# Expert tiles' down product as five fp32r products over 128 and 48 rows, the high and low parts of the 48 loaded tile by tile

## What is computed

```python
x = x + L0_ffn(L0_cond(x, itok, ...))     # top 2 of 8 experts, capacity, width 176
# second layer, on h = LoRA-SwiGLU(x) of 256 -> 1024 -> 256
probs = softmax(h @ router_w.T)                        # 16 experts
top_vals, top_idx = top_k(probs, 4)                    # normalised to sum 1
g = einsum('nh,ehi->eni', h, w_gate)                   # i = 176
u = einsum('nh,ehi->eni', h, w_up)
y = einsum('eni,eih->enh', silu(g) * u, w_down)        # the down product, 176 -> 256
routed = einsum('enh,ne->nh', y, comb)
shared = silu(h @ sh_gate) * (h @ sh_up) @ sh_down     # width 704
x = x + routed + sigmoid(h @ sh_gate_w) * shared
```

## Time and profile before

| | |
|---|---|
| three executions | 388.51, 390.02, 390.42 us (median 390.02) |
| the profiled execution | 390.62 us, of which the span is 388.8 |
| TensorE busy | 363.8 us, 94% of the span |
| VectorE busy | 227.2 us, 58% |
| GpSimd busy | 177.6 us, 46% |
| ScalarE busy | 143.4 us, 37% |
| mean granted TensorE clock | .988 of full speed |
| DMA | 53.98 MB, 139 GB/s over the span |

### The profile page before, as it was taken

One profiled execution on the slowest core, in us unless ns is written; L12 is line 12 of the kernel. 1 busy time (PEld: TensorE's weight loads), 2 busy tenths in 40 slices (PEclk: granted clock), 3 DMA queues, 4 the chain that ended last, 5 costly groups with the idle time before them and its releaser, 6 DMA issues.

```text
span 388.8 us, 6306 instructions
## 1 busy us (share of the span) xinstructions
PE 363.8 (94%) x1961; PEld 313.0 (81%) x1961; DVE 227.2 (58%) x556; ACT 143.4 (37%) x292; POOL 177.6 (46%) x162
## 2 busy tenths in 40 slices
PE   3998899999999999999999989989999999999992
PEld 3877789887888888888868768779999999999871
DVE  6796557269822222221247897775766566566696
ACT  2653466334444343333333715543222222232110
POOL 0606664566064445424222115763443344177783
PEclk9999999999999999999998999999999999999998
DMA  7985255145962134310111058752443444255633
GB/s 223 370 317 176 77 168 187 58 161 177 385 242 94 45 132 135 135 40 3 40 40 42 1 176 174 186 170 78 129 109 110 124 112 114 88 162 165 190 97 121
DMA packets 26949, 53.98 MB, mean 139 GB/s; under 512 B 4278, under 2 KB 16054, under 8 KB 26582
## 3 DMA queue, kind: packets, MB, share of 16 engines
q1 hardware_dynamic: 21686, 39.28, 30.8%
q0 software_dynamic: 5232, 14.29, 13.4%
HBM read 40.19 MB, written 15.47 MB: 143 GB/s over the span
## 4 chain that ended last, share of the span: by engine, by line
PE 73%; DVE 10%; DMA 6%; issue 3%; POOL 3%; ACT 2%; SPq 1%; POOLq 0%; DVEq 0%; ACTq 0%
PE gu L1552 10%; PE y L1944 10%; PE gu L1554 10%; PE gu L1553 10%; PE gu L1916 4%; PE gu L1920 4%; PE gu L1917 4%; PE y L1552 2%; PE y L1553 2%; PE y L1554 2%; PE gu L1578 2%; DMA xgT_f<-y_k,slot_s 2%; PE gu L1928 2%; DMA w_raw<-y_k 1%; PE gu L1865 1%
## 5 line engine op out<-in xcount | busy, mean ns | idle before, releaser
L616 POOL TENSOR_TENSOR w_lo<-w_raw,w_hi 128x768 fp32r<-128x768 f32 (+3 forms) x26 | 34.4, 1344 | 77.9 <-ACT w_hi L750 60.7
L1053 DVE TENSOR_TENSOR hid<-silu,gu 128x512 f32<-128x512 f32 x24 | 16.5, 686 | 66.1 <-PE gu L1554 66.0
L1552 PE MATMUL gu<-act_hi,w_hi 128*128 128x512 f32 x128 | 52.9, 413 | 1.5 <-DVE hid L1053 1.5
L1553 PE MATMUL gu<-act_lo,w_hi 128*128 128x512 f32 x128 | 51.0, 399 | 0.0
L1554 PE MATMUL gu<-act_hi,w_lo 128*128 128x512 f32 x120 | 48.1, 401 | 0.0
L978 ACT ACTIVATE silu<-gu 128x176 f32<-128x176 f32 x47 | 14.9, 317 | 72.2 <-PE gu L1920 72.2
L1916 PE MATMUL gu<-w_hi,xgT 128*128 x94 | 38.7, 413 | 0.8 <-ACT xgT L933 0.8
L1434 DVE TENSOR_TENSOR hid<-silu,gu 128x176 f32<-128x176 f32 x47 | 15.8, 337 | 37.5 <-ACT silu L978 34.9
L779 ACT ACTIVATE hid_hi<-hid 128x512 fp32r<-128x512 f32 x24 | 15.2, 632 | 49.1 <-DVE hid L1053 49.0
L1552 PEld LDWEIGHTS gu<-act_hi,w_hi 128*128 128x128 f32 x128 | 24.8, 194 | 7.1 <-DVE hid L1053 2.0
L1917 PE MATMUL gu<-w_lo,xgT 128*128 x94 | 30.1, 321 | 0.0
(11 more groups left out here) (354 smaller groups left out, 917.6 us busy)
## 6 DMA issues: line engine op xcount, KB each, us to landing
y_k<-w_raw SPq DMA_DIRECT2D x47, 128.0 KB, 2.2
w_raw<-in_w_gu SPq DMA_DIRECT2D x16, 352.0 KB, 4.6
w_raw<-in_wc SPq DMA_DIRECT2D x8, 576.0 KB, 4.0
w_hi_f<-in_w0s SPq DMA_DIRECT2D x6, 368.0 KB, 4.8
y_k<-hid SPq DMA_DIRECT2D x1, 2048.0 KB, 12.3
w_dn<-in_w_dn SPq DMA_DIRECT2D x1, 1936.0 KB
w_raw<-in_ws SPq DMA_DIRECT2D x5, 384.0 KB, 3.0
w_hi_f<-y_k SPq DMA_DIRECT2D x6, 256.0 KB, 4.4
```

Source lines behind the costliest of these rows:

```text
L616: nc.gpsimd.tensor_tensor(w_lo[par][:, w], w_raw[par][:, w], w_hi[par][:, w].bitcast(F32), ALU.subtract).then_inc(split, 1)
L1053: V.tensor_tensor(out[rows(tail)], silu[s][rows(tail)], up[rows(tail)], ALU.mult).then_inc(s_prod, 1)
L1552: T.matmul(out, w[0], x[0], start=start, stop=False)
L1553: T.matmul(out, w[0], x[1], start=False, stop=False)
```

## The change

The down product of a tile (176 x 256) is no longer two fp32 products over 88 rows each. The 176 rows are cut into 128 and 48. The 128 rows have a high and a low part in SBUF, side by side in lora_store, made once (by ScalarE and GpSimd, `w1_dn_high`, `w1_dn_low`), in two instructions each, of 11 and 5 experts. The 48 rows stand for each expert in a new DRAM array w1_rest of 128 rows by 256, with the high part from row 0 and the low part from row 64. It is made during COND in four pieces of four experts (`rest_load`, `rest_high`, `rest_low`, `rest_store`) in the buffers sg_b and xgT, and the piece of a tile's expert is loaded for every tile by SyncE (`rest_in`, 128 KB, the address from a register) into a ring of three and rounded by VectorE (`round_rest`) into one of two. Hidden is written by VectorE as 128 columns and, at column 128 and again 64 further, the last 48. The turned hidden part gets a high part from ScalarE (`hid_turned_high`, from PSUM) and a low part from VectorE (a subtraction, PSUM less SBUF); its ring has three places instead of four. The result is copied to t_out by ScalarE (`output`) instead of VectorE. Choice gathers open one tile earlier (Y_OPEN 31).

```diff
-Y_OPEN, Y_A_TILE = 32, 2
+Y_OPEN, Y_A_TILE = 31, 2
...
+TURNED, REST_RING, REST_BACK = 3, 3, 3
...
# SyncE
+            def rest_load(k):
+                if k:
+                    sp.wait_ge(rest_low_done, ES + k)
+                n = REST_EXP * H
+                sp.dma_start(sg_b[:], d["w1_dr"][:, k * n:(k + 1) * n]).then_inc(rest_landed, 16)
+
+            def rest_store(k):
+                sp.wait_ge(rest_low_done, ES + k + 1)
...
             for c in range(C0[COND] + 2, C0[COND] + NC[COND]):
                 cond_chunk(c, c % 2)
+                k = c - C0[COND] - 2
+                if 1 <= k <= REST_PIECES:
+                    rest_store(k - 1)
+                if k < REST_PIECES:
+                    rest_load(k)
...
+            def rest_in(i):
+                e = sp.value_load(own[0:1, i:i + 1], min_val=0, max_val=E1 - 1)
...
                 sp.dma_start(d["y_k"][i * P:(i + 1) * P], t_out[i % RING]).then_inc(s_y[i % RING], 16)
+                if i + REST_RING + 1 < SLOT_TILES:
+                    sp.wait_ge(rest_rounded, ES + i + 2)
+                    rest_in(i + REST_RING + 1)
                 if i:
                     landed(i - 1)
...
# GpSimd
+            def w1_dn_low(k):
+                of = slice(*WD_EXPERTS[k])
+                pool.wait_ge(s_w1h, NC[COND] + k + 1)
+                nc.gpsimd.tensor_tensor(w1_dn_lo[:, of], w1_dn_raw[:, of], w1_dn_hi[:, of].bitcast(F32),
+                                        ALU.subtract).then_inc(s_w1l, 1)
...
-            for i in range(9, SLOT_TILES):
+            w1_dn_low(0)
+            for i in range(9, XG):
+                gather(i, i)
+            w1_dn_low(1)
+            for i in range(XG, SLOT_TILES):
                 gather(i, i % XG)
...
# ScalarE
+                if 2 <= k < 2 + REST_PIECES:
+                    rest_high(k - 2)
...
             gu1_high(last_cols(1))
+            w1_dn_high(0)
             shared(3, 0)
             act.wait_ge(s_ids, 1)
             turned_in(0)
             shared(3, 1, lambda: turned_in(1))
+
+            w1_dn_high(1)
+
+            def hid_turned_high(i):
+                act.wait_ge(t_hT, i + 1)
+                if i >= TURNED:
+                    act.wait_ge(t_dn, i - TURNED + 1)
+                A.activation(t_hidT[i % TURNED][0], hidT_ps(i), ACT.Copy).then_inc(t_hh, 1)
...
# VectorE
+                if 2 <= k < 2 + REST_PIECES:
+                    rest_low(k - 2)
...
-                V.tensor_tensor(t_hid[i % DEPTH], t_silu[i % 2], tile_gu(i)[:, I_EXP:GU_N], ALU.mult).then_inc(t_hd, 1)
...
+                V.tensor_tensor(out[:, 0:I_EXP], t_silu[i % 2], up, ALU.mult)
+                V.tensor_tensor(out[:, P + REST_AT:P + REST_AT + I_REST], t_silu[i % 2][:, P:], up[:, P:], ALU.mult).then_inc(t_hd, 1)
...
             def turned_hidden(i):
-                dve.wait_ge(t_hT, i + 1)
-                if i >= DEPTH:
-                    dve.wait_ge(t_dn, i - DEPTH + 1)
-                V.tensor_copy(t_hidT[i % DEPTH].rearrange("p k n -> p (k n)"), hidT_ps(i)[0:HALF_I]).then_inc(t_hTs, 1)
+                dve.wait_ge(t_hh, i + 1)
+                hi, lo = t_hidT[i % TURNED]
+                V.tensor_tensor(lo, hidT_ps(i), hi.bitcast(F32), ALU.subtract).then_inc(t_hTs, 1)
+
+            def round_rest(i):
+                q = i % REST_RING
+                dve.wait_ge(s_w1[q], W1_BEFORE[q] + 32 + 16 * (i // REST_RING + 1))
+                if i >= 2:
+                    dve.wait_ge(t_dn, i - 1)
+                V.tensor_copy(rest_w[i % 2], rest_raw[q]).then_inc(rest_rounded, 1)
...
# TensorE
                 if i == 0:
-                    pe.wait_ge(s_w1d, 16 * len(WD_EXPERTS))
+                    pe.wait_ge(s_w1l, W1_SPLITS + len(WD_EXPERTS))
...
-                for k in range(2):
-                    last = T.matmul(out_ps[i % 2], t_hidT[i % DEPTH][:, k], w1_dn[0:HALF_I, bass.ds((e * 2 + k) * H, H)],
-                                    start=k == 0, stop=k == 1)
...
+                T.matmul(out_ps[i % 2], hi[:, 0:P], w_hi, start=True, stop=False)
+                T.matmul(out_ps[i % 2], hi[:, 0:P], w_lo, start=False, stop=False)
+                T.matmul(out_ps[i % 2], lo[:, 0:P], w_hi, start=False, stop=False)
+                pe.wait_ge(rest_rounded, ES + i + 1)
+                T.matmul(out_ps[i % 2], hi[:, P:2 * P], of, start=False, stop=False)
+                last = T.matmul(out_ps[i % 2], lo[0:I_REST, P:2 * P], of[0:I_REST], start=False, stop=True)
                 last.then_inc(t_dn, 1)
```

## The result

The changed kernel is slower: 412.69 us (median of four executions, 409.58 to 417.53) against 390.22, a ratio of 1.055 with a 95% interval of 1.049 to 1.061. The longest execution ran at a lower clock than the others and is left out of this ratio and its interval; it is in the median. The forecast was 389.1 and its range ended at 393.5. The profiled execution took 409.58 with a span of 407.4 us, where the one before took 390.62 and 388.8, so 19.0 us are to be found.

The account below looks back on a forecast made before the run. The prediction took TensorE to bound the kernel and summed -12.3 + .4 + .9 + 7.2 + 1.5 + .7 = -1.6 us at the end of the tiles, taken as -.9 at the kernel's end: median 389.1 us, range 384.0 to 393.5.

Parts of the forecast that it names:

- What bounds the kernel: In the expert tiles TensorE is busy 10.00 of 10.00 us, so a tile costs what its TensorE products cost.
- The gain: Tile steps: five down products at .117 take .585 instead of .87 us, 43 times: 12.3 us off (5.8 to 14.4).
- The bound of .147: Tiles: a 256-column product takes no longer than the 320-column one, .147 us.
- The lock-out: Before tile 0, GpSimd's 2816-column low part shuts out VectorE's two-input subtraction: gate/up 7.2 us later (1.9 to 7.9).
- The clock: In TensorE's gap before tile 0 it falls to 1.2 GHz and stays some 3 us with work: +1.5 (0 to 2.6).
- COND: On SyncE's queue the raw load behind the new store lands near 147, without slack: +.7 for three chunks (0 to 1.5).
- rival B: COND: VectorE loses to GpSimd in two chunks, store and load 1.7 later each: 3.7 instead of .7, 392.1; chance .17.
- ScalarE, VectorE and SyncE have cover in the steps: Tile steps: with their added work all three stay below the 1.98 us step, with about .4 us of cover.
- What ends the kernel: VectorE's adds (moving -1.6) and GpSimd's choice gathers (+.1 to +1) end together; the end moves -1.6 to 0, taken as -.9.
- The sum: All terms give -1.6 us at the end of the tiles, and -.9 at the kernel's end.

Follow-up runs that it names:

- rows_128: The changed kernel with the fifth down product over all 128 rows instead of 48: 398.89 us, 1.021 of the kernel before.
- twice_48: The changed kernel with the product over 48 rows issued twice in a row in each tile: 416.03 us, one execution.
- all_three: lock_free with ScalarE's high part of 2816 columns cut in three and put where ScalarE had waited: 388.68 us, .995 of the kernel before.
- low_after_12: The changed kernel with both of GpSimd's low parts of the down weights behind the twelfth gather: 415.57 us, 1.069 of the kernel before.
- lock_free: Changed kernel, fifth product over 128 rows, COND store and load one chunk later, GpSimd's low parts behind VectorE's last shared subtraction, larger one halved: 388.67 us, .994.
- low_eighths: all_three with GpSimd's low parts in six pieces and three gathers between them: 387.42 us, .994 of the kernel before.

## Why the prediction was wrong, point by point

- **What bounds the kernel**: right. TensorE is busy 10.00 of 10.00 in the tiles of both kernels.
- **The gain**: the price of a product was right (.117 forecast, .11 to .12 in the chain), and the step that failed is its use for all five. All five were priced by their 256 columns alone; but the product over 48 rows stands by itself between products over 128, and costs .2 more on either side. Forecast -12.3, measured 43 x (2.38 - 2.26) = +5.2, and the switch is 17 of these 17.5 us (rows_128, twice_48). The bound of .147 was too low an upper end for an operand shape that no row near it had. The trace of before holds a sign of it: its last products go in groups of eight, over 64 and over 128 rows in turn,

```profile
375.65 1.99 PE L2010 MATMUL y<-w_raw,hid 128*128 128x256 f32 x8
377.57 1.99 PE L2010 MATMUL y<-w_raw 64*128 64x256 f32 x8
379.50 1.99 PE L2010 MATMUL y<-w_raw,hid 128*128 128x256 f32 x8
```

  and each group takes 1.92 us, where eight records at the .2175 of the earlier trace rows are 1.74: .18 more for each group, and so for each change of the row count. That it is the change and not something else of these groups, no run tried.
- **The lock-out**: right in mechanism and size. 7.2 forecast from 251.78; 6.6 measured net of what came ahead of it. The lock's own share is 5.51 - .69 = 4.8 (5.3 forecast), and ScalarE's high part ahead of silu cost the 1.9 forecast, which all_three took off. low_after_12 and lock_free showed that it is a race: whoever starts first holds the other, and an operation that is moved meets the next one.
- **The clock**: right that it falls in the gap. Its price was undersized: 1.5 forecast, up to 2.7 measured, since it stayed at .50 until 267, 5.4 us of them with work and not 3.
- **COND** (rival B): the place and the order were right, the size was not. Taken at .7, measured 3.66 of waiting and 4.3 in all; rival B had 3.7. The store's time was met within .1 us; the load took 6.9 from its issue in the first of the three chunks (5.9 and 6.2 in the next two), not 5.8; for that 5.8 the prediction shows no working, and no row before had a load behind 1 MB. The rival's own mechanism, VectorE losing a race to GpSimd, played a small part: its subtraction took 1.22, 1.40, 2.07 and 2.05 us.
- **ScalarE, VectorE and SyncE have cover in the steps**: right (5.20 and 5.86 of 10 us). That the load of the 48 rows can land late was not in the sum, and made TensorE wait 2.6 us in low_eighths once the step was short.
- **What ends the kernel**: the prediction let the adds and the gathers end together, with the gathers moving by +.1 to +1. The first gather moved by 16.0 (338.06 to 354.06) and the span by 18.6, since TensorE and the adds behind it were later still.
- The sum with two terms corrected, -.9 + 43 x .4 + 3.0, gives 19.3 against 19.0 measured. That it is so close is in part luck: the clock cost more than forecast behind the gap, and the kernel before lost 1.4 at 209 to 213 that the changed one did not.

## What to carry to other kernels

Price a TensorE product by its row count as well as by its columns, and look in the trace at what a product costs at the change from one row count to another: one odd product per loop step costs two changes, and padding it to the rows of its neighbours cost nothing here. Before a long two-input operation is put on GpSimd, list all of VectorE's two-input operations in the time that it lasts; moving it only chooses another one to wait. On a queue in order, an instruction that waits for this chunk's result belongs behind the loads of the next. And before a saving per step is multiplied by all steps, look at what runs at a pace of its own beside the last of them: here the choice gathers, once open, need 50 us to the end whatever TensorE does faster.

## What the runs showed of the hardware

- The change between a product over 48 rows and one over 128 costs .2 us each way (fp32r, 256 and 352 columns); 96 rows beside 128 cost nothing, nor do fp32 products over 88 rows in the kernel before.
- The lock between VectorE and GpSimd can hold over two GpSimd instructions in a row: 8.56 us for a .69 us subtraction behind 6.2 + 2.9 us. Where a gather stood between two of them, VectorE's operation got in (low_eighths: it ended at 259.37, between subtractions that ended at 258.21 and began at 259.62).
- TensorE's clock falls to .50 with TensorE at work in some executions and not in others of the same stretch: 1.4 us lost at 209 to 213 in the kernel before, nothing there in the changed one.
- The same program, the kernel before, took 390 us (medians 389.96 to 390.22) beside the changed kernel and eight of the runs, and 412 to 414 on two other chips.
